# Merging the sheaf stage with the scatter of its messages to sources, one batch apart

## The reference

```
xs, xd = x[src], x[dst]
reflection(a, b) = relu(concat(a, b) @ W1.T + b1) @ W2.T + b2
F_s, F_d = householder(reflection(xs, xd)), householder(reflection(xd, xs))
L_sd = -einsum('eki,ekj->eij', F_s, F_d)
msg_s = coef * einsum('eij,ej->ei', L_sd, xd)
msg_d = coef * einsum('eji,ej->ei', L_sd, xs)
out = x - scatter_add(src, msg_s) - scatter_add(dst, msg_d)
```

## Time and profile before

| what | us |
|---|---|
| median of three runs | 8023.22 |
| the profiled execution | 8028.09 |
| its span, first to last instruction | 8026.3 |
| first transpose of the sheaf stage, start | 6320.7 |
| last source matmul, end | 8020.15 |

### The profile page before, as it was taken

How to read it: one execution, slowest core, us unless ns; L and a number is a source line. 1 busy time by engine, 2 the same in 40 slices (tenths; PEclk the granted TensorE clock), 3 DMA queues, 4 the chain that set the end, 5 groups by cost and what they waited for, 6 DMA issues and landing times. The chain is left out here.

```text
span 8026.3 us, 119080 instructions
## 1 busy us (share of the span) xinstructions
PE 5857.5 (73%) x33540; PEld 3931.1 (49%) x33541; DVE 5670.7 (71%) x10923; ACT 1607.1 (20%) x2670; POOL 4181.5 (52%) x4125
## 2 busy tenths in 40 slices
PE   4444442664446888877999995545899899999999
PEld 2433342554444555554555552544244466666555
DVE  5666662743336999989999999999000488888898
ACT  0111110011103555541222220441000122222000
POOL 0777774777775777775777770000000477776000
PEclk9555555555557999998999997798899655555999
DMA  3222223321122333351111110220576211111000
GB/s 112 71 67 69 69 69 80 85 50 37 38 43 56 84 85 85 84 76 40 41 41 41 41 41 22 93 102 33 220 284 263 63 33 33 31 33 29 0 0 1
DMA packets 492400, 550.24 MB, mean 69 GB/s; under 512 B 130191, under 2 KB 395399, under 8 KB 478712
## 3 DMA queue, kind: packets, MB, share of 16 engines
q1 hardware_dynamic: 349464, 483.93, 18.5%
q0 software_dynamic: 131584, 43.10, 5.8%
q10 hardware_dynamic: 11232, 21.73, 1.0%
HBM read 452.30 MB, written 96.00 MB: 68 GB/s over the span
## 5 line engine op out<-in xcount | busy, mean ns | idle before, releaser
L1307 POOL DMA_INDIRECT sh_ring<-node,sh_idx x832 | 826.0, 993 | 1594.8 <-DVE sh_idx L1997 1333.4
L1551 POOL DMA_INDIRECT slots<-rec,row x832 | 858.9, 1032 | 353.8 <-issue 274.3
L1307 POOL DMA_INDIRECT mx_ring<-node,mx_idx x832 | 856.1, 1029 | 319.9 <-issue 224.0
L938 POOL DMA_INDIRECT mid_ring<-typed,mid_idx x832 | 839.3, 1009 | 258.9 <-issue 253.3
L446 POOL DMA_INDIRECT slots<-rank_staged,rank_row_i x782 | 795.5, 1017 | 262.2 <-issue 246.8
L426 PE MATMUL rank_found<-rank_next_sb,rank_hot_hi_t 26*128 26x128 f32 x1568 | 367.5, 424 | 573.9 <-ACT rank_next_sb L408 568.5
L1657 PE MATMUL sm_sums<-sm_both,sm_hot 128*128 128x512 f32 x1664 | 784.4, 594 | 0.2 <-DVE sm_both L1578 0.2
L1147 PE MATMUL mid_sums<-mid_ring,mid_hot_d 128*128 128x17 f32 x1664 | 391.5, 375 | 419.9 <-DMA mid_ring<-typed,mid_idx 408.1
L426 PEld LDWEIGHTS rank_found<-rank_next_sb,rank_hot_hi_t 26*128 26x128 f32 x1568 | 341.4, 325 | 599.0 <-issue 591.8
L1147 PEld LDWEIGHTS mid_sums<-mid_ring,mid_hot_d 128*128 128x128 f32 x1664 | 383.4, 312 | 436.0 <-issue 436.0
L2158 PE MATMUL srl_sums<-srl_outer,srl_hot_lo 128*128 128x400 f32 x1664 | 560.5, 500 | 7.4 <-DVE srl_outer L2140 7.4
(11 more groups left out here) (406 smaller groups left out, 12100.0 us busy)
## 6 DMA issues: line engine op xcount, KB each, us to landing
strips<-near SPq DMA_DIRECT2D x100, 1562.5 KB, 8.7
mx_far<-far_row SPq DMA_DIRECT2D x208, 256.0 KB
rank_key_row<-key_rows SPq DMA_DIRECT2D x98, 512.0 KB
near<-adj_whole SPq DMA_DIRECT2D x175, 256.0 KB, 2.0
sm_low<-low_row SPq DMA_DIRECT2D x208, 128.0 KB
sh_low<-low_row SPq DMA_DIRECT2D x104, 256.0 KB, 3.3
feat_t<-mid_out ACTq DMA_DIRECT2D x104, 204.0 KB
mx_feat<-feat_t SPq DMA_DIRECT2D x208, 102.0 KB
```

The costliest lines, as they stand in the source:

```text
L938: pool.indirect_dma_start(ring[:, n % DEEP, j, 0:D], None, m.typed, bass.IndirectOffsetOnAxis(ap=idx[:, t:t + 1], axis=0)).then_inc(gather ...
L1307: pool.indirect_dma_start(ring[:, n % AHEAD, j, :], None, table, bass.IndirectOffsetOnAxis(ap=idx[:, t:t + 1], axis=0)).then_inc(gathered[ ...
L1551: pool.indirect_dma_start(m.slots2, bass.IndirectOffsetOnAxis(ap=row2[:, t:t + 1], axis=0), rec2[:, t, :], None).then_inc(m.ordered, 16)
```

## The change

`to_sources` goes away as a stage, and its work is done inside `sheaf_messages`, one batch behind. The parts are:

- VectorE's `hots` compares 16 columns of `lows` instead of 8 (destination places and source places of one batch) and writes both one-hots as bf16 into `hot_16`; ScalarE copies them to fp32 (`hot`). `hot_lo` is no longer made.
- `spread` uses the fp32 one-hot and the fp32 message, one fp32 matmul a tile; the split into `three` (four VectorE operations) goes.
- `spread_far` makes `hot_hi` (now in PSUM, in one bank with `v_ps`) and `outer` for the batch before, and `sources` does the eight matmuls of 400 columns. It stands last in TensorE's turn.
- The square goes from VectorE to ScalarE (`ACT.Square`), as does the copy of the gathered rows (`near_ends`); `coef` is computed straight from the ring. The copy to `m.parts` goes.
- `vectors` waits also for `outer` of two batches back, since `hot_hi` and `v_ps` share a bank.

```diff
@@ -1884,26 +1884,38 @@
...
-        hot, hot_t = sb("hot", [P, 2, TB // 2, P, 2], BF16), sb("hot_t", [P, TB * P], BF16)
-        lows, iota = sb("lows", [P, NT], BF16), sb("iota", [P, P, 2], BF16)
+        hi_i, lo_i, hi, real = sb("hi_i", [P, NT], I32), sb("lo_i", [P, NT], I32), sb("hi", [P, NT]), sb("real", [P, NT])
+        lows, iota = sb("lows", [P, total, 2 * TB], BF16), sb("iota", [P, P, 2], BF16)
+        hot_16, hot = sb("hot_16", [P, 2, TB, P, 2], BF16), sb("hot", [P, 2, TB, P, 2])
+        hot_t, outer = sb("hot_t", [P, TB * P], BF16), sb("outer", [P, 2, TB, NB * D])
...
-        rest, three, both = sb("rest", [P, TB, D]), sb("three", [P, 2, TB, 3 * D], BF16), sb("both", [P, 2, TB, 2, D])
+        both = sb("both", [P, 2, TB, 2, D])
         xd, et_ps, hid_ps = ps("xd", [P, TB, HW]), ps("et_ps", [2 * D, TB * P]), ps("hid_ps", [P, TB * P])
-        v_ps, sums = ps("v_ps", [P, TB, 2 * D]), ps("sums", [P, 512])
+        shared, sums, far_sums = ps("shared", [P, 512]), ps("sums", [P, 512]), ps("far_sums", [P, 512])
+        v_ps = shared[:, 0:TB * 2 * D].rearrange("q (t c) -> q t c", c=2 * D)
+        hot_hi = shared[:, 256:256 + TB * NB].rearrange("q (t s) -> q t s", s=NB)
...
-        LINKS = 17
...
+        LINKS = 10
...
         def _(pool):
-            gather(pool, m.node20, idx, ring, idx_s, gathered, ends_s, TB, total)
+            pool.wait_ge(idx_s, 1)
+            for n in range(total):
+                if n >= AHEAD:
+                    pool.wait_ge(coef_s, n - AHEAD + 1)
+                    pool.wait_ge(near_s, n - AHEAD + 1)
...
-            def spread_hots(n, h):
-                wait(dve, used, n - 1)
-                wide = [P, TB // 2, P, 2]
-                now = lows[:, bass.ds(n * TB, TB)].rearrange("q (a t) -> q a t", t=2)
-                nc.vector.tensor_tensor(hot[:, h], now[:, :, None, :].to_broadcast(wide), iota[:, None, :, :].to_broadcast(wide),
+            def hots(r):
+
+                n, h = r.n, r.mod(2)
+                wait(dve, cast_s, n - 1)
+                wide = [P, TB, P, 2]
+                now = lows[:, bass.ds(n, 1), :].rearrange("q o (a t) -> q (o a) t", t=2)
+                nc.vector.tensor_tensor(hot_16[:, h], now[:, :, None, :].to_broadcast(wide), iota[:, None, :, :].to_broadcast(wide),
                                         ALU.is_equal).then_inc(hot_s, 1)
 
             def gather_ends(r):
 
...
+                dve.wait_ge(xd_s, n + 1)
+                nc.vector.tensor_copy(ends[:, h, :, 1, :], xd[:, :, 0:D]).then_inc(ends_s, 1)
                 dve.wait_ge(gathered[slot], (r.div(AHEAD) + 1) * 16 * TB)
-                dve.wait_ge(xd_s, n + 1)
-                nc.vector.tensor_copy(ends[:, h, :, 0, :], ring[:, slot, :, 0:D])
-                nc.vector.tensor_copy(coef[:, h, :], ring[:, slot, :, D])
-                nc.vector.tensor_copy(ends[:, h, :, 1, :], xd[:, :, 0:D]).then_inc(ends_s, 1)
-                dve.wait_ge(ends_s, n + 1)
-                nc.vector.tensor_tensor(coef[:, h, :], xd[:, :, D], coef[:, h, :], ALU.mult).then_inc(vec_s, 1)
+                wait(dve, both_s, n - 1)
+                nc.vector.tensor_tensor(coef[:, h, :], xd[:, :, D], ring[:, slot, :, D], ALU.mult).then_inc(coef_s, 1)
...
+            def spread_far(r):
+
+                n, h = r.n, r.mod(2)
+                now = bass.ds(n * TB, TB)
+                wait(dve, outer_s, n)
+                nc.vector.tensor_tensor(hot_hi, hi[:, now][:, :, None].to_broadcast([P, TB, NB]),
+                                        m.iota_row[:, None, 1:NB + 1].to_broadcast([P, TB, NB]), ALU.is_equal).then_inc(hi_s, 1)
+                wait(dve, far_used, n - 1)
+                dve.wait_ge(both_s, n + 1)
+                dve.wait_ge(hi_s, n + 1)
+                nc.vector.tensor_tensor(outer[:, h].rearrange("q t (s d) -> q t s d", d=D),
+                                        both[:, h, :, 0, :][:, :, None, :].to_broadcast([P, TB, NB, D]),
+                                        hot_hi[:, :, :, None].to_broadcast([P, TB, NB, D]), ALU.mult).then_inc(outer_s, 1)
...
-                spread_hots(n, h)
+                hots(r)
                 dve.wait_ge(v_s, 2 * n + 2)
-                link(nc.vector.tensor_tensor(flat(vec), v_ps[:, :, :], m.mlp_b2[:, None, :].to_broadcast([P, TB, 2 * D]), ALU.add))
-                link(nc.vector.tensor_tensor(sq[:, :, :, :], vec[:, :, :, :], vec[:, :, :, :], ALU.mult))
-                nc.vector.tensor_reduce(norm[:, :, :], sq[:, :, :, :], AX.X, ALU.add).then_inc(norm_s, 1)
+                nc.vector.tensor_tensor(flat(vec), v_ps[:, :, :], m.mlp_b2[:, None, :].to_broadcast([P, TB, 2 * D]), ALU.add).then_inc(bias_s, 1)
                 if inside(n + 2, total):
                     far_hots(r.plus(2))
+                dve.wait_ge(sq_s, n + 1)
+                nc.vector.tensor_reduce(norm[:, :, :], sq[:, :, :, :], AX.X, ALU.add).then_inc(norm_s, 1)
+                if inside(n - 1, total):
+                    spread_far(r.plus(-1))
                 dve.wait_ge(root_s, n + 1)
                 link(nc.vector.tensor_scalar(norm[:, :, :], norm[:, :, :], 1e-12, None, ALU.max))
                 link(nc.vector.reciprocal(norm[:, :, :], norm[:, :, :]))
+                dve.wait_ge(bias_s, n + 1)
                 link(nc.vector.tensor_tensor(vec[:, :, :, :], vec[:, :, :, :], norm[:, :, :, None].to_broadcast(shape), ALU.mult))
...
+                dve.wait_ge(near_s, n + 1)
...
-                wait(dve, kept_s, n - 1)
-                link(nc.vector.tensor_tensor(both[:, h, :, :, :].rearrange("q t a d -> q t (a d)"), flat(msg),
-                                             coef[:, h, :, None].to_broadcast([P, TB, 2 * D]), ALU.mult))
                 wait(dve, used, n - 1)
-                near = both[:, h, :, 1, :]
-                link(nc.vector.tensor_copy(three[:, h, :, 0:D], near))
-                link(nc.vector.tensor_tensor(rest[:, :, :], near, three[:, h, :, 0:D], ALU.subtract))
-                link(nc.vector.tensor_copy(three[:, h, :, D:2 * D], rest[:, :, :]))
-                nc.vector.tensor_tensor(three[:, h, :, 2 * D:3 * D], rest[:, :, :], three[:, h, :, D:2 * D],
-                                        ALU.subtract).then_inc(three_s, 1)
+                nc.vector.tensor_tensor(both[:, h, :, :, :].rearrange("q t a d -> q t (a d)"), flat(msg),
+                                        coef[:, h, :, None].to_broadcast([P, TB, 2 * D]), ALU.mult).then_inc(both_s, 1)
                 if inside(n + 2, total):
                     gather_ends(r.plus(2))
...
+            spread_far(Turn((total - 1) // AHEAD, (total - 1) % AHEAD, AHEAD))
             dve.wait_ge(used, total)
...
-            def turn(q, h):
-                n = 2 * q + h
+            def near_ends(r):
+
+                n, h, slot = r.n, r.mod(2), r.mod(AHEAD)
+                act.wait_ge(gathered[slot], (r.div(AHEAD) + 1) * 16 * TB)
+                nc.scalar.copy(ends[:, h, :, 0, :], ring[:, slot, :, 0:D]).then_inc(near_s, 1)
+
+            def turn(r):
+                n, h = r.n, r.mod(2)
+                act.wait_ge(bias_s, n + 1)
+                nc.scalar.activation(sq[:, :, :, :], vec[:, :, :, :], ACT.Square).then_inc(sq_s, 1)
                 act.wait_ge(norm_s, n + 1)
                 nc.scalar.activation(norm[:, :, :], norm[:, :, :], ACT.Sqrt).then_inc(root_s, 1)
                 if inside(n + 1, total):
                     network(n + 1)
-                act.wait_ge(three_s, n + 1)
-                nc.scalar.copy(m.parts[:, bass.ds(n * TB, TB), :], both[:, h, :, 0, :]).then_inc(kept_s, 1)
-
+                act.wait_ge(hot_s, n + 1)
+                wait(act, used, n - 1)
+                wait(act, far_used, n - 1)
+                nc.scalar.copy(hot[:, h], hot_16[:, h]).then_inc(cast_s, 1)
+                if inside(n + 2, total):
+                    act.wait_ge(swap_s, 2 * n + 2)
+                    near_ends(r.plus(2))
...
             def turned_ends(n, h):
+                pe.wait_ge(near_s, n + 1)
...
-                    wait(pe, norm_s, n)
+                    wait(pe, bias_s, n)
+                    wait(pe, outer_s, n - 1)
...
-                pe.wait_ge(hot_s, n + 1)
-                pe.wait_ge(three_s, n + 1)
+                pe.wait_ge(cast_s, n + 1)
+                pe.wait_ge(both_s, n + 1)
                 for k in range(TB // 2):
                     b = blocks[k]
                     for j in (2 * k, 2 * k + 1):
-                        for part in range(3):
-                            last = nc.tensor.matmul(sums[:, bass.ds(b * D, D)], hot[:, h, k, :, j % 2],
-                                                    three[:, h, j, part * D:(part + 1) * D], start=False, stop=True,
-                                                    skip_group_check=True)
+                        last = nc.tensor.matmul(sums[:, bass.ds(b * D, D)], hot[:, h, k, :, j % 2], both[:, h, j, 1, :], start=False,
+                                                stop=True, skip_group_check=True)
```

(52 more changed lines are left out.)

68 lines of the change are left out of this document (12 added, 56 removed).

## The result

The changed kernel takes **8057.7 us** (median of 6 runs, 8048.5 to 8067.1), the kernel before 8024.2 (6 runs): ratio 1.004, interval 1.003 to 1.005. It is slower by 33 us; 8052 was predicted. Its profiled execution has a span of 8055.3 us. One fact is needed for the experiments: in the comparisons between this one and the last, on three chips, the kernel before itself took 10055 to 10197 us, so their absolute times stand only beside the kernel before of the same comparison.

A forecast was written before the change was run, and what follows sets the result against it. TensorE was taken to bound both stages, at 1.2 GHz in the sheaf stage and 2.4 in `to_sources`. Merged: 1716 (104 turns of 16.5) + 12 + 1 = 1729 against 1699.5, +29, giving 8052 us; range 7900 to 8140.

The forecast's parts named there:

- Clock, rising and falling each turn: Merged stage: clock falls after the sources and rises again in them; turn 16.5 us, main case held at 0.82.
- Sources: Source matmuls in a merged turn: 10.7 us at 1.2 GHz, first 4.25 slow, the other 6.45 in 3.2.
- The fp32 spreading: `spread` in a merged turn: taken as 3.41 us at 1.2 GHz, like `vectors`, and half at 2.4.
- Rival 3: In `spread`, strided fp32 weights load at half speed: 6.8 us at 1.2 GHz, +260 us, about 8310; chance 0.05.
- The widening: ScalarE's copy of the one-hots to fp32, 2048 elements a turn: 1.95 us, hidden under TensorE's turn.
- the seam: Junction of the sheaf and `to_sources` stages: it goes, its time being already within the 1699.5 us of before.
- the 0.46 us: TensorE's wait before `network` for the copy of the transposes: goes, since `spread` outlasts that copy.
- The 12 us: Both ends of the merged stage: TensorE waits for VectorE, 12 us together, an estimate.
- Rival 1: Merged stage stays at 2.4 GHz: TensorE's 12.1 and VectorE's 11.7 meet at about 12.5 a turn, 7637 us; chance 0.10.

The follow-up runs named there:

- Four pieces: Changed kernel with each batch's eight source matmuls cut into four pieces of two tiles, behind vectors, spreading, network and far ends: 7681.0 us, 0.957 of the kernel before.
- the spreading alone: Kernel before, two stages kept, with only the fp32 spreading: one-hot widened by ScalarE, VectorE's split gone; 1.003 of the kernel before.

## Why the prediction was right

- **Clock, rising and falling each turn: right.** 0.74 lies in 0.67 to 0.80, and sources begin at 0.50 in 102 of 104 batches. The turn is 16.40 (16.5 predicted), the stage from the first transpose to the last source matmul about 1730 (1729). Cutting the streams removed the fall, which shows that it was the cause and not only the company of the time lost.
- **That the sum came within 6 us is partly luck.** The clock rose 4.05 us into the sources (4.25 taken) and fell 3.2 to 6.5 us behind them in all but the last three batches, mean 4.4 (3.75 taken), so 7.8 us of a turn pass at 2.4 GHz and not 6.95; against that the turn's work comes to 24.2 us at 1.2 GHz (16.40 + 7.8) and not 23.5. The two nearly cancel. Single turns lie on both sides of the mean: they repeat in sixes of 14.2, 15.9 and four times 17.2 us.
- **Sources: right.** 4.25 + 3.2 = 7.45 a batch worked out, 788.8 / 104 = 7.58 measured.
- **The fp32 spreading: right in size, on the cheap side of the clock.** 3.43 a batch at 1.2 GHz against the 3.41 taken from `vectors`; in the merged kernel it stands behind the sources, mostly at 2.4 GHz, and takes 1.97. Rival 3 (6.8) is out. In the one comparison that has both, the changed kernel is 1.1% slower with it than with the bf16 form.
- **VectorE: right in sum, wrong in one wait.** 1172.48 us in 104 turns is 11.3 a turn. `outer` takes 3.49, no more than when `hot_hi` lay elsewhere. The one-hot went from 0.69 to 1.22 where 1.38 was taken. But its idle time is mostly the wait for the far ends (319 us), and only half as much for `vectors` (158), which was named: the copy of the ends stands first in its order.
- **ScalarE: right.** The widening takes 1.89 (1.95), 519.30 us in 104 turns is 5.0 a turn (5.4).
- **Waits of TensorE: none but 10.0 us** for the copy of the transposed ends in the first two batches, so the seam and the 0.46 us went as said. The 12 us were taken for both ends of the stage; at its end TensorE did not wait.
- **Rival 1 (7637 us), held at 0.10, did not happen, but what it described can be had.** Four pieces ran at 1.00 with a turn of 12.73 against its 12.5. Its 12.1 of TensorE was short by 0.6: four short streams take 1.53, 1.45, 1.43 and 1.44 us from start to start, 5.85 for what takes 5.39 in one, and spreading and network 0.1 each. Its deciding point was named rightly (the clock when the next sources begin).
- **The rule weighed there** (the Trainium skill, TensorE: Matmul & The Clock Gate, section "Why this matters for your kernels") says that a TensorE kept busy holds the full clock. Here the merged stage is busy all the time at 0.74, and a stage busy for 99% (the spreading alone) stood at 0.50 while one busy for 90%, with the extra matmuls of 256 columns in it, had 0.81: the runs contradict it.
